# Graph attention on one core: probabilities as weights, a joined positive part, and two of ten additions on TensorE

## The reference

```python
h = jnp.maximum(_layernorm(x, axis=-1), 0.0)
Wx = h @ Ws[hd] + Wb[hd]
s = Wx[dst] @ a_w[hd, :64] + Wx[src] @ a_w[hd, 64:] + a_b[hd]
s = jax.nn.leaky_relu(s, negative_slope=0.2)
alpha = _segment_softmax(s, dst, n)
out_hd = jax.ops.segment_sum(alpha[:, None] * Wx[src], dst, num_segments=n)
x = x + concatenated out_hd
```

## Time and profile before

| what | value |
|---|---|
| median of three runs | 1238.27 us (1237.48 to 1239.95) |
| profiled execution, own time | 1239.9 us |
| its span | 1238.2 us |
| mean granted clock of TensorE | 0.958 |
| the attention's stage, first product to last sum | 535 to 824 us |

### The profile page before, as it was taken

One profiled execution on the slowest core, in us unless ns is written; L12 is line 12 of the kernel. 1 busy time (PEld: TensorE's weight loads), 2 busy tenths in 40 slices (PEclk: granted clock), 3 DMA queues, 4 the chain that ended last, 5 costly groups with the idle time before them and its releaser, 6 DMA issues. The chain is left out here.

```text
span 1238.2 us, 16225 instructions
## 1 busy us (share of the span) xinstructions
PE 1132.0 (91%) x5959; PEld 714.8 (58%) x5959; DVE 914.5 (74%) x1652; ACT 716.0 (58%) x901; POOL 64.5 (5%) x117
## 2 busy tenths in 40 slices
PE   6999969996999977979999999969999999999996
PEld 4666635555785544434444444436557777777775
DVE  5999962017656697878899997865448888888885
ACT  2324846005548666058877877845137777777774
POOL 3000132000002100000000000000000000000000
PEclk9899989998999987979999999989999999999999
DMA  4000000003003000204111100000021001111002
GB/s 157 5 1 1 1 2 2 1 0 136 1 1 95 1 1 1 85 24 147 45 45 44 45 24 2 2 1 1 1 52 27 20 8 27 27 27 27 2 1 83
DMA packets 24771, 36.18 MB, mean 29 GB/s; under 512 B 11874, under 2 KB 13204, under 8 KB 24694
## 3 DMA queue, kind: packets, MB, share of 16 engines
q1 hardware_dynamic: 24694, 35.14, 9.4%
HBM read 26.03 MB, written 2.70 MB: 23 GB/s over the span
## 5 line engine op out<-in xcount | busy, mean ns | idle before, releaser
L62 PE MATMUL wide<-arena 125*125 125x512 bf16 (+5 forms) x2076 | 462.2, 372 | 16.3 <-DVE arena L962 7.5
L62 PEld LDWEIGHTS wide<-arena 125*125 125x125 bf16 (+5 forms) x2076 | 253.9, 131 | 197.9 <-issue 80.7
L1783 PE MATMUL wide<-arena 125*65 125x512 f32 (+1 forms) x480 | 182.3, 516 | 0.0
L1385 PE MATMUL wide<-ident,arena 125*125 125x125 f32 (+3 forms) x954 | 132.0, 286 | 11.6 <-ACT arena L618 4.2
L758 ACT ACTIVATE arena<-arena,b 125x1250 f32<-125x1250 f32 x80 | 106.7, 1336 | 60.1 <-PE wide L1783 55.8
L1278 DVE TENSOR_TENSOR arena<-wide,arena 125x1250 f32<-125x1250 f32 x80 | 116.7, 1459 | 31.2 <-PE wide L1773 31.1
L1385 PEld LDWEIGHTS wide<-ident,arena 125*125 125x125 f32 (+3 forms) x954 | 116.5, 187 | 21.8 <-issue 8.9
L841 ACT ACTIVATE arena<-wide 125x1000 f16<-125x1000 f32 x80 | 80.8, 1010 | 79.7 <-PE wide L1385 79.7
L1783 PEld LDWEIGHTS wide<-arena 125*65 125x65 f32 x480 | 63.4, 138 | 101.8 <-issue 95.4
L1344 DVE SCALAR_TENSOR_TENSOR arena<-wide,arena 125x1000 f16<-125x1000 f32 x80 | 95.9, 1199 | 33.6 <-ACT arena L841 33.6
L856 ACT ACTIVATE arena<-arena,neg_max,unit 125x1250 f32<-125x1250 f32 x80 | 114.3, 1429 | 5.7 <-DVE neg_max L1371 5.7
(11 more groups left out here) (255 smaller groups left out, 1260.1 us busy)
## 6 DMA issues: line engine op xcount, KB each, us to landing
arena<-rows_kept SPq DMA_DIRECT2D x16, 625.0 KB, 5.9
arena<-arena SPq DMA_DIRECT2D x40, 156.2 KB, 2.9
arena<-in_L_gnn_W SPq DMA_DIRECT2D x3, 1024.0 KB, 7.7
x_nm<-in_x SPq DMA_DIRECT2D x2, 1250.0 KB
out<-x_nm SPq DMA_DIRECT2D x1, 2187.5 KB
arena<-in_L_gnn_W_l SPq DMA_DIRECT2D x1, 1024.0 KB, 6.3
arena<-in_L_gnn_W_r SPq DMA_DIRECT2D x1, 1024.0 KB, 8.4
arena<-in_L_gnn_Wk SPq DMA_DIRECT2D x1, 1024.0 KB, 5.3
```

The costliest lines, as they stand in the source:

```text
L62: mm = pe.matmul(ps[0:rows, lo:hi], lhsT, rhs[:, lo:hi], start=start, stop=stop, skip_group_check=True)
L1385: return pe.transpose(dst, src, ident[0:k, 0:k])
L1783: m = pe.matmul(psW[1][0:VA, lo:hi], v_gat[0:ROWS, t, h, :], ring[n % RINGS][0:ROWS, lo:hi], start=(t == 0), stop=(t == TILES - 1))
```

## The change

The stage keeps its tiles, its heads and its order; four things change in it.

- **Weighing.** The 125x125 blocks of probabilities are held as weights and the 125x65 values move: ten products a tile into `small` (125 targets on partitions, ten blocks of 65). `turn_out` goes; `acc_out` is one copy of 125x650 to `o_nm`. `sums` reads that from SBUF.
- **Joined positive part.** 0.2 b + relu(0.8 t + 0.8 b) is written as b + max(0.8 t, -0.8 b). In eight tiles of ten VectorE does the maximum and the addition in one operation on `t_bc` (which now holds 0.8 t), `least08` and the product. ScalarE's positive part goes there, and its exponential has bias b.
- **Two of ten additions by TensorE.** In tiles 1 and 6 (`BY_PE`) ScalarE still makes the positive part; TensorE adds it with an f32 product with the unit matrix, and the exponential reads PSUM.
- `psW[0]` and `psW[1]` take the products in turn; a product waits for its buffer's reader two tiles back. `shift_turn` stands ahead of the product of tile 6, `shift_out` ahead of the exponential of tile 6. The addition to `x_nm` goes to GpSimd (`add_head`), but for the last head. `targets_in` waits for VectorE's operations as well.

```diff
+BY_PE = (1, 6)
...
-        o_rows = region(12500, [N])
+        o_nm = region(12500, [2, HEAD_HALF, VA])
...
-            return psW[1][0:3 * TILES, 1024:1024 + ROWS] if h == 0 else small[0:3 * TILES, 384:384 + ROWS]
+            return psW[1][0:3 * TILES, 1024:1024 + ROWS] if h == 0 else psW[0][0:3 * TILES, 1280:1280 + ROWS]
...
-                    sp.wait_ge(S["relu2_made"], TILES * h)
+                    sp.wait_ge(S["relu2_made"], by_pe(TILES * h - 1))
+                    sp.wait_ge(S["z2_made"], by_dve(TILES * h - 1))
...
+            def add_head(h):
+
+                pool.wait_ge(S["head_summed"], h + 1)
+                xs = x_nm[0:ROWS, :, DH * h:DH * h + DH]
+                pool.tensor_tensor(xs, xs, head_sum[0:ROWS, :, :, :].rearrange("p u t d -> p (u t) d"), ALU.add).then_inc(S["acc_read"], 1)
+
             for h in range(1, H):
                 shift_of(pool, done, h)
+                if h >= 2:
+                    add_head(h - 2)
             pool.wait_ge(S["w_maxed"], 3)
             pool.partition_all_reduce(w_all[:, :], w_most[:, :], 128, RMAX).then_inc(S["w_spread"], 1)
+            add_head(H - 2)
...
-                    act.activation(ring[n % RINGS][0:ROWS, :], t_bc[h % 2][0:ROWS, :], ACT.Relu, scale=0.8,
-                                   bias=b08[0:ROWS, h, t:t + 1]).then_inc(S["relu2_made"], 1)
+                    i = BY_PE.index(t)
+                    act.activation(ring[n % RINGS][0:ROWS, :], t_bc[h % 2][0:ROWS, :], ACT.Relu,
+                                   bias=b08[0:ROWS, h, i:i + 1]).then_inc(S["relu2_made"], 1)
 
                 def acc_out(h):
 
-                    after(act, "turned2", h)
-                    for c, (lo, hi) in enumerate(PIECES):
-                        act.wait_ge(*((S["acc2_full"], 2 * h + c + 1) if c < 2 else (S["used2"], TILES * (h + 1))))
-                        copy(o_rows[0:VA, lo:hi], psW[1][0:VA, lo:hi]).then_inc(S["acc2_out"], 1)
+                    act.wait_ge(S["used2"], TILES * (h + 1))
+                    after(act, "acc_read", h)
+                    copy(o_nm[0:ROWS, :, :, :], acc_view(small)).then_inc(S["acc2_out"], 1)
...
-                positive_part(0)
-                positive_part(1)
+                for n in range(2):
+                    if n in BY_PE:
+                        positive_part(n)
                 for n in range(H * TILES):
                     h, t = divmod(n, TILES)
-                    if n + 2 < H * TILES:
+                    if n + 2 < H * TILES and (n + 2) % TILES in BY_PE:
                         positive_part(n + 2)
-                    act.wait_ge(S["z2_made"], n + 1)
                     row = ring[n % RINGS][0:ROWS, :]
-                    act.activation(row, row, ACT.Exp, bias=b02[0:ROWS, h, t:t + 1]).then_inc(S["exp2_made"], 1)
+                    if t in BY_PE:
+                        act.wait_ge(S["masked2"], n + 1)
+                        if t == BY_PE[1] and h + 1 < H:
+                            shift_out(h + 1)
+                        i = BY_PE.index(t)
+                        act.activation(row, psW[n % 2][0:ROWS, 0:N], ACT.Exp, bias=b02[0:ROWS, h, i:i + 1]).then_inc(S["exp2_made"], 1)
+                    else:
+                        act.wait_ge(S["z2_made"], by_dve(n))
+                        act.activation(row, row, ACT.Exp, bias=b10[0:ROWS, h, t:t + 1]).then_inc(S["exp2_made"], 1)
                     if t == 1 and h >= 1:
                         acc_out(h - 1)
-                    if t == 6 and h + 1 < H:
-                        shift_out(h + 1)
...
-            def sums(h, signal, steps):
-
-                dve.wait_ge(S[signal], steps)
-                acc = acc_view(small)
+            def sums(h):
+
+                dve.wait_ge(S["acc2_out"], h + 1)
+                after(dve, "acc_read", h)
                 rd = rden[0:ROWS, :]
                 rd2 = rd.rearrange("p (u t) -> p u t", u=2)
-                done(ts(rd2, acc[:, :, :, DH], TINY, None, ALU.max))
+                done(ts(rd2, o_nm[0:ROWS, :, :, DH], TINY, None, ALU.max))
                 done(dve.reciprocal(rd, rd))
-                done(tt(head_sum[0:ROWS, :, :, :], acc[:, :, :, 0:DH], rd2.unsqueeze(3).to_broadcast([ROWS, 2, HEAD_HALF, DH]), ALU.mult))
-                xs = x_nm[0:ROWS, :, :].rearrange("p t (h d) -> p t h d", h=H)[:, :, h, :]
-                tt(xs, xs, head_sum[0:ROWS, :, :, :].rearrange("p u t d -> p (u t) d"), ALU.add).then_inc(S["acc_read"], 1)
+                mean = tt(head_sum[0:ROWS, :, :, :], o_nm[0:ROWS, :, :, 0:DH], rd2.unsqueeze(3).to_broadcast([ROWS, 2, HEAD_HALF, DH]), ALU.mult)
+                if h < H - 1:
+                    mean.then_inc(S["head_summed"], 1)
...
-                dve.tensor_copy(tcol[0:ROWS, :, :], cols[:, 0:H, :])
-                ts(b08[0:ROWS, :, :], cols[:, H:2 * H, :], 0.8, None, ALU.mult)
-                ts(b02[0:ROWS, :, :], cols[:, H:2 * H, :], 0.2, None, ALU.mult).then_inc(S["cols_out"], 1)
+                ts(tcol[0:ROWS, :, :], cols[:, 0:H, :], 1.25, None, ALU.mult)
+                dve.tensor_copy(b10[0:ROWS, :, :], cols[:, H:2 * H, :])
+                ts(least08[0:ROWS, :, :], cols[:, H:2 * H, :], -0.8, None, ALU.mult)
+                few = cols[:, H:2 * H, BY_PE[0]::BY_PE[1] - BY_PE[0]]
+                ts(b08[0:ROWS, :, :], few, 0.8, None, ALU.mult)
+                ts(b02[0:ROWS, :, :], few, 0.2, None, ALU.mult).then_inc(S["cols_out"], 1)
...
-                    row = ring[n % RINGS][0:ROWS, :]
-                    dve.wait_ge(S["masked2"], n + 1)
-                    dve.wait_ge(S["relu2_made"], n + 1)
-                    tt(row, psW[0][0:ROWS, 0:N], row, ALU.add).then_inc(S["z2_made"], 1)
+                    h, t = divmod(n, TILES)
+                    if t not in BY_PE or h == H - 1:
+                        dve.wait_ge(S["masked2"], n + 1)
+                    if t not in BY_PE:
+                        if t == 0:
+                            dve.wait_ge(S[f"tb{h % 2}_in"], 16 * (h // 2 + 1))
+                        after(dve, "used2", n - RINGS + 1)
+                        stt(ring[n % RINGS][0:ROWS, :], t_bc[h % 2][0:ROWS, :], least08[0:ROWS, h, t:t + 1], psW[n % 2][0:ROWS, 0:N],
+                            ALU.max, ALU.add).then_inc(S["z2_made"], 1)
                     if n + LEAD < H * TILES:
                         largest_source(n + LEAD)
                     if n % TILES == 4 and n >= TILES:
-                        sums(n // TILES - 1, "turned2", n // TILES)
+                        sums(n // TILES - 1)
...
+                    ps = psW[n % 2]
                     if t % HEAD_HALF == 0:
                         pe.wait_ge(S["shift_hi_in" if t else "shift_lo_in"], 16 * (h + 1))
                     if n == 0:
                         pe.wait_ge(S["lo_made2"], TILES)
-                    after(pe, "z2_made", n)
+                    if n >= 2:
+                        pe.wait_ge(*((S["exp2_made"], n - 1) if (n - 2) % TILES in BY_PE else (S["z2_made"], by_dve(n - 2))))
+                    if t == BY_PE[1] and h + 1 < H:
+                        shift_turn(h + 1)
                     for lo, hi in PIECES:
-                        pe.matmul(psW[0][0:ROWS, lo:hi], sel_w[:, 0:ROWS], ln_hi[:, t, lo:hi], start=True, stop=False)
+                        pe.matmul(ps[0:ROWS, lo:hi], sel_w[:, 0:ROWS], ln_hi[:, t, lo:hi], start=True, stop=False, skip_group_check=True)
                     for lo, hi in PIECES:
-                        m = pe.matmul(psW[0][0:ROWS, lo:hi], ident_neg[0:ROWS, 0:ROWS], ln_lo[0:ROWS, t, lo:hi], start=False, stop=True)
+                        m = pe.matmul(ps[0:ROWS, lo:hi], ident_neg[0:ROWS, 0:ROWS], ln_lo[0:ROWS, t, lo:hi], start=False, stop=t not in BY_PE,
+                                      skip_group_check=True)
+                    if t in BY_PE:
+                        pe.wait_ge(S["relu2_made"], by_pe(n))
+                        for lo, hi in PIECES:
+                            m = pe.matmul(ps[0:ROWS, lo:hi], ident[0:ROWS, 0:ROWS], ring[n % RINGS][0:ROWS, lo:hi], start=False, stop=True,
+                                          skip_group_check=True)
                     m.then_inc(S["masked2"], 1)
 
                 def weigh2(n):
 
                     h, t = divmod(n, TILES)
                     pe.wait_ge(S["exp2_made"], n + 1)
-                    for c, (lo, hi) in enumerate(PIECES):
-                        if t == 0 and h >= 1:
-                            pe.wait_ge(S["acc2_out"], 3 * (h - 1) + c + 1)
-                        m = pe.matmul(psW[1][0:VA, lo:hi], v_gat[0:ROWS, t, h, :], ring[n % RINGS][0:ROWS, lo:hi],
-                                      start=(t == 0), stop=(t == TILES - 1))
-                        if t == TILES - 1 and c < 2:
-                            m.then_inc(S["acc2_full"], 1)
+                    if t == 0:
+                        after(pe, "acc2_out", h)
+                    for j in range(TILES):
```

(3 more changed lines are left out.)

41 lines of the change are left out of this document (22 added, 19 removed).

## The result

The change made the kernel slower: 1248.24 us (median of 5, 1245.94 to 1255.25) against 1239.28 us (median of 5), ratio 1.0092 with a 95% interval of 1.0056 to 1.0129. The forecast was 1251 us, with a range of 1244 to 1264.

The account below looks back on a forecast made before the run. TensorE was taken as the bound, VectorE 10% behind. Heads 1 to 5, 6, 7, 0, then ahead of and behind the stage: 15.7 - 0.8 + 0.8 - 2.6 + 0.3 - 0.9 = +12.5 us on 1238.27, so 1251; range 1244 to 1264.

Parts of the forecast that it names:

- The bound: Attention heads: TensorE is the bound and stays busy throughout; VectorE falls from 30.30 to 27.4 us a head.
- The weighing: Weighing on TensorE: 20 instructions a tile at 0.109 us, 2.18 us, 0.09 more a tile than before.
- the lower end of 0.104: Weighing instruction's low estimate, loads scaled down with their columns and no fixed part: 0.104 us, -8 us in the sum.
- The additions: Tiles 1 and 6 on TensorE: two f32 unit-matrix additions a head, +4.18 us; sixteen in all, 33 us.
- The middle heads: Heads 1 to 5: 33.67 us becomes 36.8 us each, +3.1 a head, +15.7 us together.
- Head 6: Head 6 of the attention: from 37.64 us to 36.8, -0.8 us, as VectorE now has time for its searches.
- head 7: Last head, to the end of its last weighing: from 42.4 us to 43.2, +0.8 us.
- Head 0: First head: from 36.38 us to 33.8, -2.6 us, with the clock up by 541; +2.2 if low until 551.
- The ends: Ahead of the stage two small VectorE operations, +0.3 us; behind it `turn_out` and two of three copies go, -0.9 us.
- weights in series: Rival, weighing: full-row loads cannot overlap the product before, 0.163 us an instruction, 1337 us; chance 0.02.
- The columns pace: Rival, weighing: loads are hidden, 0.054 us an instruction, VectorE becomes the bound, some -46 us, 1192; chance 0.04.
- The clock and the small gaps: Rival, TensorE: head 0 stays slow, changes of form cost gaps, instructions take 0.113 us; 1255 to 1266 us; chance 0.13.

Follow-up runs that it names:

- e1: The changed kernel itself, run once more: 1249.83 us, 1.0081 of the kernel before.
- e6: The changed kernel with 33 moving columns in place of 65 in each weighing product: 1254.25 us in one run.
- e7: The changed kernel with 63 weight columns in place of 125 in nine of ten tiles' weighing: 1205.66 us in one run.
- e9: e2 with probabilities and values of the weighing in f16, one instruction a product in place of two: 1197.57 us, 0.9681 of the kernel before.
- e2: The changed kernel with no tile added by TensorE, VectorE doing the joined operation in all ten: 1218.24 us, 0.9840 of the kernel before.
- e8: e2 with the product's wait put back to the tile before, as if one buffer took the products: 1231.28 us, 0.9934 of the kernel before.

## Why the prediction was right

The time (1251 for 1248.24 and, in e1, 1249.83) and the sign are right, and so is the mechanism: 33 us of additions on the bound, and less given back than they cost. That the time came out within 3 us is in part luck, since single executions lie from 1246 to 1255; the stage is the better measure, +9.6 us with its end where the forecast's parts have +12.2. The steps one by one:

- **The bound.** TensorE is busy in the whole of each head, as forecast, and VectorE stands at 27.28 us (forecast 27.4).
- **The weighing.** Forecast 0.109 us an instruction from the weight loads of the earlier trace rows and 2.18 us a tile. The distance within a weighing is 0.109, and a weighing takes 2.14 us, since its second instruction starts 0.07 us behind the first. +0.05 a tile, not +0.09. That the load paces it was an inference from rows 7 and 8; e6 and e7 show it. Rows 8 alone could not have: the transpositions there move 125 columns, which at the old weighing's rate (2.09 us for 2500) would take 0.104 us as well. And no row stands behind the lower end of 0.104: the 0.113 of 128 columns, scaled down, is 0.110. The Trainium skill ("TensorE: Matmul & The Clock Gate", LDWEIGHTS) gives P/1.2 ns, by which 125 columns are an estimated 104 ns and 63 columns 52.5. The trace has 109 for 125 columns, 5 ns more; for 63 it has 58, which need not be the load's own time, as said at e7; and in e9, with f16 weights, the same 125 columns went by every 58 ns, under the page's 104. In time, the page's figure would have made the sum 8 us less, the row's was 3 us too high.
- **The additions.** Forecast 2.09 us each, 33 us in all; measured 2.11 each, and 31.8 us of the stage in e2, head 0's 1.8 hidden microseconds left out.
- **The middle heads.** 36.66 for 36.8. Two deviations nearly cancel in it: the tiles are 3.20 us and not 3.25, and what is left over beside ten tiles and two additions (32.0 + 4.2) is 0.44 us and not 0.1. The waits behind `sums` did go, but the shift's product lengthens tile 5 to 3.47:

```profile
619.27 0.70 PE L1820 MATMUL wide<-arena,sel_w 128*125 128x512 bf16 x3
...
620.35 2.30 PE L1838 MATMUL small<-arena 125*125 125x65 f32 x20
622.58 0.23 PE L1771 MATMUL wide<-ident_bf,parts 125*30 125x125 bf16 x1
622.74 0.75 PE L1820 MATMUL wide<-arena,sel_w 128*125 128x512 bf16 x3
```

- **What the parts gave.** e2 and e8 split the rest of the change: against the 284.4 us of before the new weighing with one buffer stands at 278.6 (-5.8; the joining and GpSimd's addition are in it), with two buffers at 263.4 (-15.2 more), and the two additions put 31.8 back.
- **Head 6** is 36.66 us (forecast 36.8) and **head 7** 43.06 to the end of its last weighing (784.37 to 827.43; forecast 43.2). The wait of head 6 quoted as 2.62 us is the product's own; the earlier trace rows shows that of its weight load, 3.03. The product's row is

```profile
762.67 0.61 PE L1771 MATMUL wide<-arena,sel_w 128*125 128x512 bf16 x1 [2.62 <-DVE arena L1278]
```

- **Head 0** took 32.45 us for 33.8: the clock was up at 535.5 (0.52 of full speed ahead of it, 1.00 behind it), earlier than the 541 that I took. TensorE worked without a gap from 531.97 on, as forecast. But in e8, with one buffer and no additions, the clock stayed at half through 14.2 us without a gap, and the same head took 40.57 us; that the clock rises behind such work was right here and is no rule.
- **The ends.** Behind the stage -1.1 for -0.9. Ahead of it +0.3 was forecast; the profiles differ by -3.2 and +4.0 us there, which hides it.
- **ScalarE's copy** took 0.71 us (0.7 forecast) and was hidden; GpSimd's addition 1.55 us in six heads and 2.69 in one (L556, mean 1.71), not 1.4, and hidden too; the joined operation 1.515 us, where the addition took 1.459 and I had priced the two alike.

Together: the stage and its end gave +9.6 us; without the 0.3 us ahead of the stage the forecast's parts sum to +12.2. The difference is 1.3 in head 0, 0.8 in heads 1 to 6, and the rest in head 7 and the end.

The rivals: *weights in series* would have been 0.163 us an instruction; it was 0.109, and stayed so in e6 with half of the stream, so load and stream do not add up; the 512-column f32 instructions of the addition hide their loads altogether (six in 2.11 us). So the rule of the Trainium skill ("TensorE: Matmul & The Clock Gate", Part 3) by which a load overlaps only with other row groups does not hold in these traces: all of these have the same rows. *The columns pace* is refuted by e6. *The clock and the small gaps* did not come: the clock was up early, and a tile of 3.20 us is 1.06 + 2.14 with nothing between them.

## What to carry to other kernels

Before work is moved between engines, take one period of the stage and write down each engine's busy time in it: what is put on the engine that fills the period costs its full time (2.10 us for each of the 14 additions of heads 1 to 7 here), and what is taken from the others gives back only the waits that they caused. A change of several parts can hide a good one: the same change without its additions takes 1.6% less than the kernel before, and with an f16 weighing as well, whose rounding must be acceptable, 3.2%. An f32 product that is narrow on the moving side is paced by its weight load (0.109 us for 125 weight columns with 65 or 33 moving), so count weight columns and not moved ones. In f16 the same 125 weight columns went by at 0.058 us (e9).
